# First chunk's tiles split into two 16-bit parts before TensorE turns them over

## The reference, cut to what matters

```python
xn = _layernorm(x, axis=-1)                       # over 2048 channels
r = sigmoid(einsum('bsd,hd->bsh', xn, Wa) + ba)   # D = 2048
i = sigmoid(einsum('bsd,hd->bsh', xn, Wx) + bx)
a = exp(-8.0 * softplus(-Lam) * r)
u = sqrt(1.0 - a ** 2) * (i * xn)
y = scan(h = a * h + u)                           # along the tokens
h = einsum('nd,erd->ner', xn, A)                  # 8 experts of rank 64
ffn = (h @ B of the best expert) / 64 * weight    # router: softmax(xn @ Wr.T)
out = x + y + ffn
```

## Time and profile before

| | |
|---|---|
| runs shown | 1627.21, 1629.58 (median), 1822.25 us |
| the profiled execution | 1628.9 us, its slowest core's span 1627.0 us |
| spans of the 8 cores | 1617.5 to 1627.0 us |
| TensorE busy | 1567.0 us (96%) |
| VectorE busy | 1075.6 us (66%) |
| ScalarE busy | 697.6 us (43%) |
| GpSimd busy | 102.5 us (6%) |
| chain that ended last | TensorE 75%, VectorE 12%, DMA 5%, issue 5%, ScalarE 2% |
| mean granted TensorE clock | 0.995 |

### The profile page before, as it was taken

One profiled execution on the slowest core, in us unless ns is written; L12 is line 12 of the kernel. 1 busy time (PEld: TensorE's weight loads), 2 busy tenths in 40 slices (PEclk: granted clock), 3 DMA queues, 4 the chain that ended last, 5 costly groups with the idle time before them and its releaser, 6 DMA issues.

```text
span 1627.0 us, 21800 instructions; the slowest of 8 cores (1617.5 to 1627.0 us)
## 1 busy us (share of the span) xinstructions
PE 1567.0 (96%) x7488; PEld 733.5 (45%) x7488; DVE 1075.6 (66%) x1439; ACT 697.6 (43%) x946; POOL 102.5 (6%) x188
## 2 busy tenths in 40 slices
PE   3999999999999999999998999999999999999997
PEld 2554544444444444444443354444444444444443
DVE  5687649686868676756566965838374747465656
ACT  4644453534353525343433436353534343434442
POOL 0100010001010101000000001000000000000000
PEclk9999999999999999999999999999999999999999
DMA  7501264555464556533346224432323233332331
GB/s 243 143 35 53 78 180 145 149 169 175 150 158 157 154 150 170 154 115 126 105 137 178 74 85 125 135 122 90 123 86 110 100 112 108 100 120 94 116 115 52
DMA packets 74220, 202.99 MB, mean 125 GB/s; under 512 B 9728, under 2 KB 10112, under 8 KB 74112
## 3 DMA queue, kind: packets, MB, share of 16 engines
q1 hardware_dynamic: 54288, 136.40, 28.5%
q0 software_dynamic: 18816, 65.02, 11.7%
q10 hardware_dynamic: 1008, 0.18, 0.1%
HBM read 168.01 MB, written 33.55 MB: 124 GB/s over the span
## 4 chain that ended last, share of the span: by engine, by line
PE 75%; DVE 12%; DMA 5%; issue 5%; ACT 2%; SPq 1%; DVEq 0%; ACTq 0%
PE pb L95 75%; DVE ch L95 4%; DVE ring L95 2%; DVE wf L95 2%; DMA aux<-x 2%; DMA wf<-xnd 2%; DVE st L95 1%; DMA xh<-x 1%; ACT ch L95 1%; SPq L93 1%; DVE xl L95 1%; DMA wf<-x 0%; ACT xh L95 0%; DVEq L91 0%; ACT ring L95 0%
## 5 line engine op out<-in xcount | busy, mean ns | idle before, releaser
L95 PE MATMUL pb<-xh,ring 128*128 128x512 f16 x3824 | 1155.5, 379 | 5.9 <-DVE ch L95 3.7
L95 PE MATMUL pb<-xl,ring 128*128 128x512 f16 x1912 | 725.5, 379 | 0.0
L95 PEld LDWEIGHTS pb<-xh,ring 128*128 128x128 bf16 x3824 | 374.8, 98 | 459.0 <-issue 12.4
L95 ACT ACTIVATE ring<-wf 128x1024 bf16<-128x1024 f32 x224 | 232.6, 1049 | 232.0 <-DVE wf L95 122.4
L95 PEld LDWEIGHTS pb<-xl,ring 128*128 128x128 bf16 x1912 | 187.3, 98 | 222.9 <-issue 1.0
L95 DVE TENSOR_TENSOR ring<-wf,ring 128x1024 bf16<-128x1024 f32 x224 | 271.7, 1218 | 20.6 <-ACT ring L95 20.5
L95 DVE TENSOR_TENSOR ch<-ch,pb 128x512 f32<-128x512 f32 x176 | 116.7, 683 | 157.5 <-ACT ch L95 86.7
L95 PE MATMUL pb<-ring,btb 128*128 128x512 bf16 x768 | 175.9, 379 | 0.0
L95 DVE TENSOR_TENSOR wf<-wf 128x1024 f32<-128x1024 f32 (+1 forms) x144 | 166.4, 1160 | 8.5 <-DVE wf L95 5.5
L95 ACT ACTIVATE ch<-pb 128x512 f32<-128x512 f32 x110 | 64.3, 594 | 210.8 <-PE pb L95 210.7
L95 DVE TENSOR_TENSOR btb<-ch,btb 128x512 bf16<-128x512 f32 x34 | 23.5, 692 | 162.3 <-ACT btb L95 162.3
(11 more groups left out here) (104 smaller groups left out, 833.7 us busy)
## 6 DMA issues: line engine op xcount, KB each, us to landing
wf<-wu SPq DMA_DIRECT2D x128, 512.0 KB, 4.8
ring<-hgd POOLq DMA_DIRECT2D x64, 512.0 KB, 4.7
ch<-xT SPq DMA_DIRECT2D x64, 256.0 KB, 7.1
out<-ch POOLq DMA_DIRECT2D x56, 256.0 KB, 4.6
ch<-btu SPq DMA_DIRECT2D x32, 256.0 KB, 2.7
aux<-x SPq DMA_DIRECT2D x32, 256.0 KB, 4.2
aux<-xT SPq DMA_DIRECT2D x32, 256.0 KB, 5.5
xnd<-aux POOLq DMA_DIRECT2D x32, 256.0 KB, 2.7
```

Source lines behind the costliest of these rows:

```text
L95: i = calls[it[1]]()(*it[2], **it[3])
```

## The change

Each piece of a tile is first normalized in place in its landing buffer (f32, ACT), then cast from there into an f16 part in `xn_tile(..., 0)` (ACT), and the rest of it is subtracted into a second f16 part `xn_tile(..., 1)` (DVE, a new function `norm_lo`). Both parts lie in the bytes that the f32 tile had. `transposed` issues eight f16 products against an f16 identity, two for each 128 tokens, that add up in PSUM. A landing buffer is free after the subtraction. The written order moves: `norm_lo(i - 1)` follows `norm_tile(i)`; the loads of tiles 5 and 6 are issued one tile later; the loads of tile 7 move from n = 2 to n = 3, its statistics from n = 3 to n = 4 and its normalization from n = 4 to n = 5; the hand-over of `wf0` to `wf3` moves to n = 6.

```diff
+    id16_ok = DVE.op("copy", id16[:], ident[:], after=[id_ok])
...
-    def xn_tile(tb, i, hf):
+    def xn_tile(tb, i, hf, lo):
         t = (xh if i < 2 else xl)[XN[tb][hf]]
-        return bass.AP(t, 0, [[4096, 128], [1, 4096]]).bitcast(F32).rearrange(
-            "p (k c) -> p k c", k=8)[:, :, (i % 2) * 128:(i % 2) * 128 + 128]
+        return bass.AP(t, (i % 2) * 256 + lo * 128, [[4096, 128], [512, 8], [1, 128]])
...
         for h in range(2):
+            v = land_at(2 * i + h)
+            t = ACT.op("activation", v, v, AF.Identity, scale=rsx[:, i:i + 1],
+                       bias=nbx[:, i:i + 1], after=[r])
+            xn_ok[i // 4, i % 4, h] = [
+                ACT.op("activation", xn_tile(i // 4, i % 4, h, 0),
+                       v.rearrange("p (k c) -> p k c", k=8), AF.Copy, after=[t])]
+
+    def norm_lo(i):
+        for h in range(2):
             p = 2 * i + h
-            t = ACT.op("activation", xn_tile(i // 4, i % 4, h),
-                       land_at(p).rearrange("p (k c) -> p k c", k=8),
-                       AF.Identity, scale=rsx[:, i:i + 1], bias=nbx[:, i:i + 1],
-                       after=[r])
+            v = land_at(p).rearrange("p (k c) -> p k c", k=8)
+            ok = xn_ok[i // 4, i % 4, h]
+            ok.append(DVE.op("tensor_tensor", xn_tile(i // 4, i % 4, h, 1), v,
+                             xn_tile(i // 4, i % 4, h, 0), ALU.subtract,
+                             after=list(ok)))
...
-                land_free[LF[p]] = [t]
-            xn_ok[i // 4, i % 4, h] = t
+                land_free[LF[p]] = ok
...
         for i in range(4):
-            p = PE.op("matmul", bank[b][:, ks(i)],
-                      xn_tile(tb, i, kt // 8)[:, kt % 8, :], ident[:],
-                      start=True, stop=True, skip_group_check=True,
-                      after=[id_ok, xn_ok[tb, i, kt // 8], bank_free[b]], inc=(i == 3))
+            for j in range(2):
+                p = PE.op("matmul", bank[b][:, ks(i)],
+                          xn_tile(tb, i, kt // 8, j)[:, kt % 8, :], id16[:],
+                          start=(j == 0), stop=(j == 1), skip_group_check=True,
+                          after=[id16_ok, xn_ok[tb, i, kt // 8], bank_free[b]],
+                          inc=(i == 3 and j == 1))
...
-                if 1 <= n < 5:
-                    norm_tile(3 + n)
-                if n == 2:
+                if n in (1, 2, 3, 5):
+                    norm_tile({1: 4, 2: 5, 3: 6, 5: 7}[n])
+                if n in (2, 3, 4, 6):
+                    norm_lo({2: 4, 3: 5, 4: 6, 6: 7}[n])
+                if n == 3:
                     land_load(14)
                     land_load(15)
-                if n < 4:
-                    tile_sums(4 + n)
+                if n in (0, 1, 2, 4):
+                    tile_sums({0: 4, 1: 5, 2: 6, 4: 7}[n])
...
         norm_tile(i)
-        if i < 2:
-            land_load(10 + 2 * i)
-            land_load(11 + 2 * i)
+        if i > 0:
+            norm_lo(i - 1)
+        if 0 < i < 3:
+            land_load(8 + 2 * i)
+            land_load(9 + 2 * i)
+    norm_lo(3)
```

## The result

| | before | changed |
|---|---|---|
| median of the runs | 1631.46 us | 1661.26 us |
| ratio, 95% interval | | 1.0166 [1.011, 1.0223] |
| profiled execution | 1628.9 us | 1659.78 us |
| TensorE busy | 1567.0 us | 1580.1 us |
| VectorE busy | 1075.6 us | 1093.8 us |

In some runs a whole die is granted a mean clock under 0.94; the medians keep these runs, while the ratios and the **counted** runs further down leave them out, and the ratios also every run over 1.5% above the fastest.

The account below looks back on a forecast made before the run. Up to about 137 us TensorE waits on loads, ScalarE and VectorE; afterwards its own work bounds the kernel. Head +14.8, half clock +0.7, faster turning -4.0 give +11.5 on 1628.9: 1640 us, range 1630 to 1649.

Parts of the forecast that it names:

- given back up to the softmax, less the half clock: From `x_second0(0)` to TensorE's last piece: nine faster blocks give 4.0 us, half speed in `h_step(7)` costs 0.7.
- behind the softmax: After TensorE's unbroken stretch begins, both traces run in step; nothing there gives time back.
- full-clock effect: Sum for the whole kernel: +14.8 + 0.7 - 4.0 = +11.5 us.
- The clock: Restarts at half speed after waits are hidden in the head, except behind `x_second0(0)`, where TensorE goes on 15.5 us later.
- Head: Start up to `x_second0(0)`: added ScalarE and VectorE work, 18 us each, makes TensorE wait; that copy starts 14.8 us later.
- the 14.8: ScalarE's copy of the first block of `x_second0(0)` starts at 81.2 us against 66.46, 14.8 us later.
- the 35.25: Time in us when TensorE gets tile 3's first piece, against 29.42 before: 5.8 us later.
- give-back: Between `x_second0(0)` and TensorE's last piece, nine blocks turned faster at 0.44 us each return 4.0 us.
- f16 blocks that save less: Rival, chance 0.14: turned blocks save less, so the 4.0 us shrinks, to nothing at the upper bound: 1644.4 us.
- A hidden tile 7: Rival, chance 0.12: tile 7's delay in the head is mostly hidden, its load taking 4 us: 1630 to 1636 us.
- TensorE's own work: Rival, chance 0.06: idle time absorbs the backlog, only 5.8 us stays and all 32 blocks save 14.2: 1620.5 us.
- More stalls: Rival, chance 0.12: half-speed restarts after longer waits, late `combos` sets and a later load give 1645 to 1655 us.

Follow-up runs that it names:

- e3_turn: Kernel before, order kept, x as one half-scale f16 part turned twice by eight f16 products; chip 8, undisturbed cores 0 to 3: 1619.2 us against 1624.7.
- e1_order: Kernel before with only the change's written order, f32 tiles and turning kept; chip 8, undisturbed cores 0 to 3: 1625.8 us against 1624.7.
- e4_again: The change itself run again against the kernel before; chip 8, undisturbed cores 0 to 3: 1638.0 us against 1624.7.

## Why the prediction was wrong

| step | said | measured |
|---|---|---|
| a block of eight f16 products | 0.45 us | 0.44 |
| tile of four operations on ScalarE | 4.67 us | 4.57 (13.07 to 17.64) |
| first block's last tile reaches TensorE | 35.25 | 35.06 |
| TensorE's waits for the router's weights, for block 6, for `x_second0(0)` | some 5 each | 5.10, 2.00, 5.01 |
| tile 7's load in use | 66.35 | 66.30 |
| tile 7 normalized from | 72.7 | 71.39 |
| copy of `x_second0(0)` | 81.2 | 79.7 to 80.5 on the 8 cores |
| given back up to the softmax, less the half clock | 3.3 | 4.4 (4.0 of it up to the copy of `x_second0(3)`) |
| copy of `x_second0(3)` | near 118 | 115.0 to 116.9 at full clock, 120.0 to 121.7 at 0.81 |
| last unbroken stretch of TensorE begins | 148.5 | 138.10 (core 0), 100.01 (core 5) |
| behind the softmax | unchanged | 3.2 longer |
| full-clock effect | +11.5 | +15.0 (first chip), +14.4 (chip 11), +13.3 (chip 8) |
| slowest core | 1640 | 1661.26, and 1644.24 on chip 11 |

**The step that failed is "The clock".** It took the clock to have two levels and said that the lower one would be hidden in the new head. It missed that cores may be granted 0.81 for 160 us. On the cores that had it, the router's softmax starts at 196.9 to 199.6 us against 184.5 to 186.4 on the others, 13 us later, and they end 15 us later (1652.3 against 1637.3 us on average). No more is lost than that because VectorE is still the slower one from 120 to 155 us: the copies stay 8.4 us apart on both kinds of core. 1641.9 for the slowest full-clock core and 16 us for the spell make the 1658.1 of the profile. No row of before had it. A range from that trace could not hold it. On chip 11, where it did not come, 1644.24 us lie within the range of 1630 to 1649, though the change costs 3 us more at full clock than was forecast. What sets it off stays open.

**The middle of the prediction held.** Head and turning were right as mechanisms and nearly in size. The head was put too low: I had measured it against core 1 of before, the one core whose tile 7 was latest. The copy was at 60.6 to 66.5 us on the 8 cores of before, 63.9 on average, and at 80.2 after: 16.3. Worst core against worst core, the 14.8 was right (14.1). The steps up to the 35.25 hold a slip that did no harm: 31.4 + 1.25 + 0.09 + 1.05 + 1.22 is 35.01, and the trace has 3.86 us from the start of tile 3 to that product (31.20 to 35.06) where the four terms give 3.61.

The give-back was underestimated too (e3_turn 5.5, not 4.0), and not all of it lies where the prediction had it. On cores 0 to 3 of e3_turn the copy of `x_second0(0)` comes 2.9 us earlier than in e1_order (61.8 against 64.7), in the head, where the prediction let the turning give nothing; 3.6 us more come up to the copy of `x_second0(3)`, and 0.5 up to the softmax. In the change TensorE's last stretch begins one set of VectorE's earlier than I had it; chain of core 0:

```profile
138.10 43.11 PE pb L95 x232
```

That is 22.15 us behind the copy of `x_second0(3)`, on core 1 of before 30.55. But from that copy to the end of the stretch both take about as long (65.3 and 65.8 us), so this is worth one block, as the prediction had counted.

**Behind the softmax** I had said that both would run in step. They don't quite: full-clock cores take 3.2 us longer from there to the end. From 190 us on, the waits of TensorE over 0.4 us sum to 13.6 us on average over cores 0, 1, 6 and 7 before and to 17.9 after, with the differences in waits for VectorE's `ch` and for loads; core 1 alone has hardly any (16.0 and 17.0). Why was not tested. The terms as measured, 16.3 - 4.4 + 3.2 = 15.1, meet the 15.0 of the full-clock cores, so the forecast of 11.5 was low in head and end and gained a little by the give-back.

**The rivals.** f16 blocks that save less: refuted, at 0.89 as at 0.8 and at 0.65 (a block takes 0.44 us). A hidden tile 7: refuted (its load in use at 66.30). TensorE's own work: refuted (the copy at 80, not before 70). "More stalls" had the right sign and 1645 to 1655, but by another mechanism than it named, and the measured time lies above it too.

## What to carry to other kernels

Work added in a head that another engine waits for can cost its full length, even on engines that are busy for only 43% and 66% of the span; here some 18 us on each of two engines cost 18 us, and halving the price of the products that it served gave 5.5 to 5.9 back. Compare all cores, not the slowest one, before explaining a difference: the first view here split 30 us into 15 that the change costs at full clock and 15 of a clock that some chips give and others don't. And take the price of a head from the mean of the cores if its waits are for loads.

## What the runs showed of the hardware

- TensorE was granted 0.81 of the clock, beside its two levels, in two forms: one spell of about 160 us beginning 46, 66 or 189 us into the kernel (first chip; first chip and chip 14; chip 9), or short ones of 4 to 18 us, many on one die of chip 8 and a few on chip 11. Cores 0 and 1, 2 and 3, and so on have it together; a pair may have it while the other pair of the die does not.
- It depends on the data: on cores 4 to 7 of chip 8 the same products of chunk 0 ran at a mean clock of 0.99 with data from one f16 part and 0.94 with both (cores 4 and 6 of e3_turn and e4_again).
- The Trainium skill (TensorE: Matmul & The Clock Gate, "Seeing it yourself") describes a limiter that takes a whole die to 13/16 of the clock (0.81) when a third core starts dense products, for as long as the load lasts, and that depends on the data. The value and the dependence on data agree with these runs. The rest does not: it came to pairs, the long spell ended after 160 us with the load unchanged, and on chip 11 eight dense cores had 0.81 for no more than 15 us at a time.
- A subtraction of 128x1024 (f16 from f32 and f16) took 1.22 us on VectorE and 2.12 on GpSimd.
